# The last layer norm's subtract and multiply moved from GpSimd to ScalarE in a graph attention block

## The reference

```python
q, k, v = (qkv[0], qkv[1], qkv[2])                       # x @ w_qkv, split into 8 heads
attn = jnp.einsum('bhnd,bhmd->bhnm', q, k) * scale
attn = jnp.where(attn_mask[None, None] == 0, -jnp.inf, attn)
attn = jax.nn.softmax(attn, axis=-1)
o = jnp.einsum('bhnm,bhmd->bhnd', attn, v).transpose(0, 2, 1, 3).reshape(b, n, d)
o = o @ w_proj + b_proj
ln = (o - mu) * jax.lax.rsqrt(var + LN_EPS) * ln_gamma + ln_beta
x = _layernorm(x + o + ln, axis=-1)                      # (x - m) / sqrt(v + eps): the last norm
```

## Time and profile before

| | us |
|---|---|
| median of 3 runs | 3419.73 |
| lowest and highest | 3418.71 and 3422.11 |
| the profiled execution | 3413.86 |
| its span (first to last instruction) | 3412.1 |
| PE, DVE, ACT, POOL busy | 3074.4, 2300.3, 2543.0, 2719.3 |

### The profile page before, as it was taken

The page is one execution under the profiler, slowest core; times in us unless marked ns, Lnnn a source line. Parts: engine busy times, 40 slices in busy tenths (PEclk is TensorE's granted clock), DMA queues, the critical chain, the costliest instruction groups (busy, mean ns, idle before and its releaser), DMA issues.

```text
span 3412.1 us, 123185 instructions
## 1 busy us (share of the span) xinstructions
PE 3074.4 (90%) x42624; PEld 1911.3 (56%) x42624; DVE 2300.3 (67%) x4883; ACT 2543.0 (75%) x3723; POOL 2719.3 (80%) x1543
## 2 busy tenths in 40 slices
PE   6889999898998999999898998999999998998984
PEld 3555555555555555555555555556555555555552
DVE  5556667666766767767667766767676676776764
ACT  5777777777777777777787777777777787777770
POOL 3657878787887878878788887878878788887884
PEclk9999999999999999999999999999999999999997
DMA  8999999999999999999999999999999899999992
GB/s 210 179 164 181 201 182 204 187 202 189 190 204 179 206 183 202 205 177 205 183 202 194 193 203 184 207 182 202 202 181 201 179 201 196 192 201 184 207 194 72
DMA packets 2220430, 649.09 MB, mean 190 GB/s; under 512 B 2168146, under 2 KB 2168146, under 8 KB 2220372
## 3 DMA queue, kind: packets, MB, share of 16 engines
q1 hardware_dynamic: 2166372, 548.15, 86.5%
q10 hardware_dynamic: 54000, 100.16, 10.4%
HBM read 77.60 MB, written 33.55 MB: 33 GB/s over the span
## 4 chain that ended last, share of the span: by engine, by line
POOL 51%; issue 36%; SPq 8%; PE 1%; DVE 1%; DMA 1%; POOLq 1%; ACT 1%; ACTq 0%; DVEq 0%
POOL p_lo L713 45%; SPq L271 7%; POOL x_res L723 2%; POOL norm L729 2%; POOL norm L726 2%; PE proj L361 1%; DMA pt<-p_lo 1%; POOL x_res L732 1%; POOLq L712 0%; DMA x_in<-in_x 0%; ACT p L469 0%; DMA pt<-in_adj 0%; PE side L343 0%; DVE proj L650 0%; DVE x_res L655 0%
## 5 line engine op out<-in xcount | busy, mean ns | idle before, releaser
L713 POOL TENSOR_TENSOR p_lo<-p,p_hi 128x1024 f16<-128x1024 f32 x1024 | 2174.5, 2136 | 618.8 <-ACT p_hi L482 617.7
L469 ACT ACTIVATE p<-p,row_min 128x1024 f32<-128x1024 f32 x1024 | 1174.0, 1147 | 599.2 <-DVE row_min L608 598.7
L482 ACT ACTIVATE p_hi<-p 128x1024 f16<-128x1024 f32 x1024 | 1048.0, 1044 | 63.4 <-DMA pt<-p_lo 62.4
L398 PE MATMUL pv_bank<-v_both,pt 128*128 128x64 f16 x8192 | 836.3, 194 | 34.5 <-DMA pt<-p_lo 17.5
L400 PE MATMUL pv_bank<-v_both,pt 128*128 128x64 f16 x8192 | 837.0, 194 | 0.0
L399 PE MATMUL pv_bank<-v_both,pt 128*128 128x64 f16 x8192 | 837.0, 194 | 0.0
L398 PEld LDWEIGHTS pv_bank<-v_both,pt 128*128 128x128 f16 x8192 | 745.1, 99 | 131.0 <-issue 53.5
L608 DVE CUSTOM_DVE_ANT_0 p<-scores_a,mask_q 128x1024 f32<-128x1024 f32 x512 | 623.7, 1218 | 252.6 <-PE scores_b L379 204.5
L399 PEld LDWEIGHTS pv_bank<-v_both,pt 128*128 128x128 f16 x8192 | 734.6, 99 | 82.5 <-issue 3.0
L400 PEld LDWEIGHTS pv_bank<-v_both,pt 128*128 128x128 f16 x8192 | 735.3, 99 | 0.0
L608 DVE CUSTOM_DVE_ANT_0 p<-scores_b,mask_q 128x1024 f32<-128x1024 f32 x512 | 624.0, 1219 | 0.3 <-POOL p_lo L713 0.3
(11 more groups left out here) (68 smaller groups left out, 5144.6 us busy)
## 6 DMA issues: line engine op xcount, KB each, us to landing
x_res<-in_x ACTq DMA_DIRECT2D x128, 256.0 KB, 3.3
out<-x_res ACTq DMA_DIRECT2D x128, 256.0 KB, 3.2
x_in<-in_x ACTq DMA_DIRECT2D x63, 512.0 KB, 4.6
pt<-p_hi SPq DMA_TRANSPOSE x1024, 3.4
pt<-p_lo SPq DMA_TRANSPOSE x1024, 3.5
pt<-in_adj SPq DMA_DIRECT2D x8, 512.0 KB, 9.6
ot<-in_L_gnn_w_qkv SPq DMA_DIRECT2D x4, 768.0 KB, 8.7
x_in<-in_x SPq DMA_DIRECT2D x4, 512.0 KB, 7.3
```

Of the source, the lines that this page charges most:

```text
L398: nc.tensor.matmul(o, hi, v_hi, start=(kt == 0 and ab == 0), stop=False, skip_group_check=True)
L469: nc.scalar.activation(p32[:, slot, :], p32[:, slot, :], ACT.Exp, bias=row_min[:, slot:slot + 1], scale=-1.0, accum_out=row_sum[:, head:he ...
L482: nc.scalar.activation(p_hi[:, head % RING, :], p32[:, head % RING, :], ACT.Copy).then_inc(hi_done, 1)
L713: nc.gpsimd.tensor_tensor(p_lo[:, slot, :], p32[:, slot, :], p_hi[:, slot, :], ALU.subtract).then_inc(lo_done, 1)
```

## The change

The pass over 128 x 512 leaves POOL. POOL now computes one column, minus the mean times the inverse deviation (new tile shift2, new semaphore shifted, part `shift` in the slots 29 and 45 where `out` was). ACT does the pass: Identity with that column as bias and the inverse deviation as scale, in slots 30 and 46 (slot 14 of the next group), behind everything else of that slot but the loads and stores. It waits for `shifted` and gives `out_ready`, for which the store waits as before.

```diff
-               "eps2": 28, "power2": 29, "out": 29},
+               "eps2": 28, "power2": 29, "shift": 29, "out": 30},
...
-               "eps2": 43, "power2": 45, "out": 45}]
+               "eps2": 43, "power2": 45, "shift": 45, "out": 46}]
...
+        shift2 = sb("shift2", [P, 2], F32)
...
+            def last_norm(g, i):
+                if not active(g, "P0"):
+                    return
+                wait_alone(act, shifted, projected(g, i) + 1)
+                nc.scalar.activation(x_res[:, i, :], x_res[:, i, :], ACT.Identity, bias=shift2[:, i:i + 1],
+                                     scale=norm2[:, i:i + 1]).then_inc(out_ready, 1)
...
+                    for i in range(2):
+                        for bg, bs in slot_before(g, s):
+                            if bs == NORM_SLOTS[i]["out"]:
+                                last_norm(bg, i)
                     if s == 1:
                         load_next(g)
...
                     wait_alone(pool, power_b, n + 1)
-                    nc.gpsimd.tensor_scalar(xr, xr, mv2[:, i, 0:1], norm2[:, i:i + 1], ALU.subtract, ALU.mult
-                                            ).then_inc(out_ready, 1)
+                    nc.gpsimd.tensor_scalar(shift2[:, i:i + 1], mv2[:, i, 0:1], norm2[:, i:i + 1], -1.0, ALU.mult, ALU.mult
+                                            ).then_inc(shifted, 1)
...
-                        for part in ("power", "power2", "out"):
+                        for part in ("power", "power2", "shift"):
```

More of the change, by code:

```diff
@@ L214, in attention_block @@
         stat_a, stat_b, power_a, power_b = sem("stat_a"), sem("stat_b"), sem("power_a"), sem("power_b")
-        scaled, summed, out_ready = sem("scaled"), sem("summed"), sem("out_ready")
+        scaled, summed, shifted, out_ready = sem("scaled"), sem("summed"), sem("shifted"), sem("out_ready")
         block = ctx.enter_context(nc.Block())
```

## The result

The changed kernel took 3387.8 us (median of 4 runs, 3378.51 to 3394.78) against 3419.22 for the kernel before on the same chip (4 runs, 3414.19 to 3422.11): ratio 0.9907, interval 0.9886 to 0.9928. On another chip, with new runs of both, it was 3384.72 (4 runs) against 3419.01 (15 runs).

The account below looks back on a forecast made before the run. The loop of scores on PE, minimum on DVE and exponential on ACT was taken as the bound. Savings 9.1 (SP) + 2.0 + 0.7 + 0.5 (end) = 12.3 us gave 3407.4 us against the median 3419.73; range 3391 to 3424.

Parts of the forecast that it names:

- What sets the pace: Attention groups: the loop of scores on PE, minimum on DVE, exponential on ACT bounds them, 48.1 us per ordinary group.
- DVE's 48.4 us of waits for POOL: Score loop: 38 waits under POOL's p_lo, taken as really PE's; rival reading that they are real: 3360 us, chance 0.03.
- (a): POOL loses the last norm pass, 128 times 2078 ns; in ordinary units worth nothing by itself.
- (b): POOL's new product of two 128x1 columns was taken to cost 0.42 us.
- (c): ACT's new 128x512 pass, 128 times: 0.73 us each, fitting idle times of 1.10 and 0.89 us, so costing 0.
- rival 4: ACT's room at half 1 is too small: slower, up to 16 us at its bound, 3423 us; chance 0.09.
- (d): SP's queue in transposing groups: earlier low parts remove a stall in the second following group, 0.65 a batch, 9.1 us.
- a meeting of two transfers: Ordinary groups: half 0's residual load and unit 0's low part meet; with SP's backlog, up to 0.8 us a group.
- Rival 2: SP's queue: both stalls of each batch go, saving 22 us instead of 9.1, 3394 us; chance 0.10.
- (e): Kernel's end: DVE's add waits less 2.0, last normalisation 0.7, SP's lead in the last attention group 0.5 us.
- Rival 5: POOL's new product costs as much as its old pass: 46 us slower, 3462 us, cost beginning at 1.3; chance 0.03.

Follow-up runs that it names:

- after: The changed kernel as first profiled, in an execution of 3378.51 us, the lowest of its four; median 3387.8 us.
- twice1: Changed kernel with a second ACT pass, into a spare tile, ahead of half 1's; 13 us more than the changed kernel's 3387.8.
- half0_act: Kernel before with only half 0's last norm pass given to ACT, POOL keeping half 1's; gained 7 to 8 us.
- before: The kernel before the change as profiled, in an execution of 3413.86 us; median 3419.22 us.
- after_again: The changed kernel run and profiled once more, unaltered, on another chip; 3384.72 us against 3419.01 for the kernel before.
- delay_xt0: Changed kernel with a spare POOL pass only behind half 0 in transposing groups, 14 of 128 places; cost about 20 us of the gain.
- no_pass: Kernel before with POOL's last norm pass cut to one column and no ACT pass; ratio interval 0.9859 to 0.9927.
- delay_not_xt0: Changed kernel with a spare POOL pass in 112 of 128 places, none behind half 0 of transposing groups; 3410.2 us.
- before_load11: Kernel before with half 0's residual load issued two slots later; time moved 7 us, ratio interval ending at 0.9999.
- twice0: Changed kernel with a second ACT pass, into a spare tile, ahead of half 0's; 17 us more than the changed kernel's 3387.8.

## Why the prediction was right or wrong

**What sets the pace**: right. PE's wait for row_min is the same, no ordinary group is below 48.06, POOL's relief went into its idle time (184 us more, some 200 forecast), ACT's wait for row_min fell by 75 us (90 forecast). DVE's 48.4 us of waits for POOL were a wrong name: they are 0.3 now, and its waits for PE went from 204.5 to 250.2.

**(a), (b)**: POOL's product took 0.264 us, not 0.42; both are below the point where anything waits.

**(c)**: right, with 0.802 us a pass and 0.71 from start to start for 0.73. One pass left 0.21 us before the exponential that had 0.89 idle (at 1598.89 in after). ACT waited for POOL's column 54.9 us in all, but 54.7 of that behind the start of group 63, where ACT has little else to do. What was wrong is what I said a lack of room would cost: "one for one, from 0.89 us on" (rival 4). At half 1 twice1 overran it by 0.4 us and the group kept its length.

The Trainium skill ("ScalarE: Activation LUTs", What ACT_TABLE_LOAD costs) gives 186 ns + 0.833 ns a column + about 93 ns for each column operand, 799 ns here as an estimate by that page. The trace agrees: 802.

**(d)**: this step failed. "Having lost that pause, SP is as far behind in the third group as now, so it keeps its wait" treats SP's backlog as fixed and the stall as a meeting of two transfers that a lead only shifts. The lead itself was right, to a tenth: at unit 7 of the transposing groups SP's lag fell from 1.92 to 0.20 us, 1.7 as forecast. But the lag is a running sum. SP gains or loses the difference between its own time for 32 transfers and the group's 48.07 us, and that difference changes sign: +0.8 a group when SP is behind (48.9), -0.2 on the average of the three when it is not (47.9). I had counted two pauses, L732 of half 0 only. POOL's L732 of half 1, at unit 3, put SP behind again in every group, as half0_act shows; taking it away too is what lets SP stay on time. SP's row of waits, off which I had read where POOL feeds SP, is blind to it, because a late SP does not wait there. And I counted two stalls a batch; the transposing group's own unit 3 has a third. 9.1 us became 26.7. Rival 2 had the outcome (all stalls go) at a chance of 0.10, with a price of 22 that left out the third. The meeting of the two transfers was real as a part of the stall, 1.6 of the 3.7 us by which the low part came later than now; as the whole of it, it was wrong. I also took ACT's 62.4 us as all of one kind; 29.0 of it lay in the first eight groups and stayed.

One sign of this step came out wrong as well: SP's wait for p_lo was to fall below 10 us and fell from 38.8 to 23.9. The part that I had named, behind half 0's pass (32.7 us), fell to 7.4; the rest are short waits of an SP that is now early enough to wait.

**(e)**: 3.2 us forecast, 9.0 in the first profile and 3.6 in the second. DVE's wait for L723 is gone, and the last pass is 0.26, a hop and 0.81 in place of 2.08. Much of the rest goes with PE's clock. The windows from group 63 to the end in before, after and after_again (length, PE, PEld, DVE, ACT and POOL busy, PEclk, DMA share, GB/s):

```profile
3272.70:3412.10 139.40, 81.76 (x875) 45.56 (x874) 73.11 (x161) 41.28 (x59) 88.22 (x63) 0.84 0.61 117
```

```profile
3246.40:3376.70 130.30, 76.91 (x875) 44.14 (x874) 72.84 (x161) 49.53 (x70) 66.39 (x63) 0.88 0.63 124
```

```profile
3246.90:3382.60 135.70, 82.90 (x875) 45.45 (x874) 72.72 (x161) 49.65 (x70) 66.52 (x63) 0.84 0.62 118
```

At the same granted clock as before (0.84, some 43 us at the lower level in both), after_again's end is 3.6 us shorter, close to the 3.2 of the sum. The first profile had 31 us at the lower level, and the other 5.4 us. delay_xt0 runs the changed program in its end and needed 139.0 us, with 50 us at the lower level. That is one pair at an equal clock; whether the change favours the shorter end, or it fell so twice (no_pass 129.8), stays open.

**Rival 5** fell as expected: no table loads around the passes (one in the whole run, as before), and the product far below 1.3 us.

**The time** lies 3.2 us below the range, and the range's lower end was rival 2 with its third stall missing.

## What to carry to other kernels

A queue that runs at its capacity turns a short pause into a lasting lag. Compare its own busy time plus its gaps with the period of the loop, and count how often it waits for the engine that feeds it: few such waits (50 of 1024 here, 149 without the backlog) mean a backlog, and then a pause upstream costs its consumers later, somewhere else, until something resets the lag. The same backlog hides the pause: the late queue does not wait where it is made late.
Price such a relief over all places that can make the queue late, together: one of two removed gave a quarter, both gave all. And when a wait seems to come from two transfers meeting, move one of them first, and look what it meets then: here both the wait and the meeting only moved.

## What was not expected of the hardware

- POOL's L732, a `tensor_scalar` with two column operands, takes 2078 ns for 512 columns and 383 ns for one (no_pass): (2078 - 383) / 511 = 3.3 ns a column. Its two-input additions and subtractions cost 1.7 ns a column. The product of two columns, L744, takes 264 ns.
- SP's 32 transposing transfers of an ordinary group took 41.8 us (mean) when issued on time; with SP behind they took 42.2 us (delay_not_xt0) to 43.2 (before_load11), the same transfers from the same tiles.
- A transposing group of after takes either 57.81 us or about 60. In the long ones PE's granted clock falls to 0.50, the level of 1.2 GHz, for 3.4 to 6.8 us, and unit 4 takes 15.3 us (14.8 in one) instead of 13.2. Two windows of after, the same unit in a short and in a long group:

```profile
2260.00:2264.00 4.00, 2.48 (x16) 1.68 (x16) 2.28 (x5) 1.85 (x4) 0.71 (x1) 1.00 0.32 61
...
2465.00:2469.00 4.00, 2.23 (x10) 1.10 (x10) 2.73 (x6) 2.25 (x4) 0.99 (x1) 0.50 0.17 66
```

  Unit 4 was above 14 us in 8 of 13 transposing groups before, 7 after, 12 in twice1 and 13 in twice0. In after_again and no_pass long and short groups take turns nearly throughout, and in twice0, where nothing stalls, all are long. It is the largest part of the spread between executions that I can name (2.1 us each), and what makes it come and go was not tried.
